# A feed-forward, attention, feed-forward kernel: expert and router products from scaled fp16 parts, norm statistics moved to GpSimd, and every engine's order rewritten

## The reference

```python
x = x + 0.5 * ffn(layernorm(x))        # x: 4 x 1024 x 128, f32
x = x + attn(layernorm(x))
x = x + 0.5 * ffn(layernorm(x))

def ffn(t):                            # 8 experts of 128x128, top 2
    probs = softmax(t @ router_w.T + router_b)
    w = top2(probs) / (sum of the two + 1e-10)
    y_all = einsum('nh,ehd->ned', t, experts)        # every expert
    out = sum over the two chosen of w * y_all / sum(w)
    return out * (1 + sum(w) * 1e-10)

def attn(t):                           # 8 heads of 128, 2 groups of 4 heads, latent keys and values of 32
    q = t @ wq;  k = (t @ wk_down) @ wk_up;  v = (t @ wv_down) @ wv_up
    return softmax(causal(q @ k.T / sqrt(128))) @ v @ wo
```

## Time and profile before

| | |
|---|---|
| median of 3 runs (lowest, highest) | 480.3 us (479.63, 483.49) |
| the profiled execution: its own time, its span | 482.28 us, 480.5 us |
| mean granted PE clock | 0.968 of full speed |
| busy: PE, DVE, ACT, POOL | 439.5, 398.5, 332.2, 300.4 us |

### The profile page before, as it was taken

How to read it: one execution, slowest core, us unless ns; L and a number is a source line. 1 busy time by engine, 2 the same in 40 slices (tenths; PEclk the granted TensorE clock), 3 DMA queues, 4 the chain that set the end, 5 groups by cost and what they waited for, 6 DMA issues and landing times.

```text
span 480.5 us, 10127 instructions
## 1 busy us (share of the span) xinstructions
PE 439.5 (91%) x3294; PEld 241.9 (50%) x3294; DVE 398.5 (83%) x1320; ACT 332.2 (69%) x748; POOL 300.4 (63%) x323
## 2 busy tenths in 40 slices
PE   1796989999899999999999999999899999999962
PEld 0572545444444555645655664655445545543641
DVE  5777799999979889989998988997788898933774
ACT  3356628568588756987986857984895596889433
POOL 3177005249739743697779846597497229999855
PEclk9978889999999999999999999999999999999977
DMA  6100311104001100001120100011011000000001
GB/s 193 35 21 26 83 34 39 34 2 105 2 2 52 35 1 1 2 12 43 33 67 8 34 1 3 29 46 34 13 40 57 1 25 2 1 23 1 24 7 37
DMA packets 21124, 14.52 MB, mean 30 GB/s; under 512 B 2952, under 2 KB 20944, under 8 KB 21072
## 3 DMA queue, kind: packets, MB, share of 16 engines
q1 hardware_dynamic: 21072, 13.88, 10.7%
HBM read 3.78 MB, written 2.10 MB: 12 GB/s over the span
## 4 chain that ended last, share of the span: by engine, by line
PE 69%; DVE 10%; POOL 8%; issue 6%; ACT 4%; DMA 1%; SPq 0%; POOLq 0%; ACTq 0%; DVEq 0%
PE bank L1209 11%; PE bank L1232 11%; PE bank L1254 11%; PE bank L1162 5%; PE bank L1259 5%; PE bank L1163 4%; PE bank L1164 4%; PE bank L1276 3%; PE bank L1180 3%; PE bank L1237 2%; PE bank L1134 2%; POOL sums L620 2%; POOL pair_sum L591 2%; PE bank L1150 2%; PE bank L1173 2%
## 5 line engine op out<-in xcount | busy, mean ns | idle before, releaser
L740 ACT ACTIVATE prob<-bank,exp_scale 128x512 f32<-128x512 f32 x288 | 190.5, 692 | 48.4 <-PE bank L1237 33.4
L620 POOL TENSOR_TENSOR sums<-sums,prob 128x1024 f32<-128x1024 f32 x48 | 112.9, 2372 | 0.7 <-ACT prob L740 0.7
L705 ACT ACTIVATE scaled<-bank,gate 128x128 f32<-128x128 f32 x256 | 80.5, 378 | 42.4 <-PE bank L1164 17.5
L1232 PE MATMUL bank<-q_stack,k_stack 98*128 98x512 f16 (+3 forms) x384 | 103.7, 328 | 3.6 <-DMA q_stack<-mT_lo 1.8
L1209 PE MATMUL bank<-k_stack,q_stack 96*128 96x512 f16 (+3 forms) x384 | 102.2, 329 | 1.7 <-DVE m_fin L956 1.2
L591 POOL TENSOR_TENSOR pair_sum<-dve_sum,scaled 128x256 f32<-128x256 f32 x64 | 46.8, 731 | 74.9 <-DVE dve_sum L943 63.8
L963 DVE TENSOR_REDUCE m_part<-bank 128x1 f32<-128x512 f32 x128 | 83.2, 676 | 5.7 <-PE bank L1209 5.2
L959 DVE CUSTOM_DVE_ANT_0 masked<-bank,mask_qk 128x384 f32<-128x384 f32 (+1 forms) x128 | 76.1, 612 | 5.2 <-PE bank L1209 4.6
L1254 PE MATMUL bank<-prob,v_lat 128*32 128x512 f32 (+3 forms) x768 | 78.4, 492 | 0.1
L1162 PE MATMUL bank<-we_hi,xT_hi 128*128 128x512 f32 x128 | 66.6, 520 | 1.0 <-DVE k_lo L808 0.6
L574 POOL TENSOR_TENSOR rstd<-var_eps,half_power 128x4 f32<-128x4 f32 (+1 forms) x18 | 22.1, 1226 | 64.0 <-DVE neg_mean L857 64.0
(11 more groups left out here) (129 smaller groups left out, 673.3 us busy)
## 6 DMA issues: line engine op xcount, KB each, us to landing
q_stack<-q_hi SPq DMA_DIRECT2D x32, 128.0 KB, 3.0
x<-in_L_attn_x SPq DMA_DIRECT2D x8, 256.0 KB, 3.3
q_stack<-q_lo SPq DMA_DIRECT2D x16, 128.0 KB, 3.2
out_x<-x SPq DMA_DIRECT2D x8, 256.0 KB, 2.3
k_stack<-k_hi SPq DMA_DIRECT2D x16, 64.0 KB, 2.5
we<-in_L_ffn_expert_weights SPq DMA_DIRECT2D x1, 512.0 KB, 4.1
x<-in_L_attn_wq SPq DMA_DIRECT2D x1, 512.0 KB, 6.2
x<-in_L_attn_wo SPq DMA_DIRECT2D x1, 512.0 KB, 7.4
```

The source lines that it names most:

```text
L620: nc.gpsimd.tensor_tensor(into, first if j == 1 else into, new, ALU.add).then_inc(sum_step, 1)
L705: nc.scalar.activation(scaled[:, tile % NTB, i, :], home_of(("y", f, n, 2 * t))[:, i * D:(i + 1) * D], ACT.Copy, scale=gate_of(f, n, t)[:, ...
L740: nc.scalar.activation(prob[:, n % NP, :], bank[ST + n % NST][:], ACT.Exp, scale=exp_scale[:, 0:1]).then_inc(p_ready, 1)
L1232: last = mm(into[:, at:at + CH - off], k_stack[:, b % 2, g, j * P:(j + 1) * P], q_stack[:, c, g * NR + r, off:CH], start=at == 0, stop=not ...
```

## The change

Four things are changed together.

1. The experts' weights and the router's are divided by a unit (their largest absolute value over 16384), the transposed activations (`xn` now holds half the normalised value) are multiplied by 2048, and both are split in two fp16 parts instead of two f32r parts. The triplet stays three products, now fp16; the router becomes three products for each of its four groups in place of two f32 ones. The units are found at the start in 8 new DVE steps (`weight_units`, letter `w`) and 2 new PE steps (`u`), and go back into the result through `y_unit` and `logit_unit`.
2. Of the 7 DVE steps of a norm run 2 stay (the sums); POOL does 7 (`normalisation`) in place of 2.
3. Routing has 23 steps in place of 27, writes its transpose to PSUM, and `merge` is a reduction over one operand. After this no recurring DVE step reads two operands from SBUF, apart from one-column scalars; `low_weights` at the start still does.
4. All five order strings are new. Counts of steps other than the above are the same.

The diff, cut to its core:

```diff
--- before.py
+++ after.py
@@ constants @@
+X_SCALE = 1024.0
+W_SCALE = 16384.0
-STAT_STEPS = 7
-GATE_STEPS = 27
+STAT_STEPS = 2
+NORM_STEPS = 7
+GATE_STEPS = 23
+WEIGHT_STEPS = 8
@@ the five order strings; PE_ORDER ends so @@
-    "1SSVSSz5SSY7SSSVSSY5Sl0SVSSVSV6VVY1Y2Y3Y7J6JJJY5Y0Y1Y2Y3z6l7Y0Y5Y1Y6Y3Y2Y7Y0"
+    "Y5SSVSSVl7SSVSSVSSVSSV1VVY0Y6Y2Y5Y3J1JJJY0Y6Y2Y5Y1Y3Y7Y0z6Y2l1Y5Y6Y3Y7Y0Y2Y1Y5"
@@ buffers @@
-        we_hi = sb("we_hi", [P, NE * D], F32R)
-        we_lo = sb("we_lo", [P, NE * D], F32R)
+        we_hi = sb("we_hi", [P, NE * D], FP16)
+        we_lo = sb("we_lo", [P, NE * D], FP16)
+        rw_hi = sb("rw_hi", [P, DL], FP16)
+        rw_lo = sb("rw_lo", [P, DL], FP16)
-        xT_hi = sb("xT_hi", [P, 4, CH], F32R)
-        xT_lo = sb("xT_lo", [P, 4, CH], F32R)
+        xT_hi = sb("xT_hi", [P, 4, CH], FP16)
+        xT_lo = sb("xT_lo", [P, 4, CH], FP16)
@@ GpSimd: norm_power becomes normalisation @@
-            def norm_power(l, n, chunks, i):
+            def normalisation(l, n, chunks, now):
                 at, run = norm_tiles(l, n, chunks), runs(l, n)
-                if i == 0:
+                g = nc.gpsimd
+
+                def step(i, after, op, *args, **kw):
+                    if i == now:
+                        if after is None:
+                            pool.wait_ge(bn_done[l], (n + chunks) * TC)
+                        else:
+                            pool.wait_ge(norm_step[l], (run - 1) * NORM_STEPS + after + 1)
+                        op(*args, **kw).then_inc(norm_step[l], 1)
+
+                mean_e, mean_o = (stats[:, l, at, k] for k in (1, 4))
+                df, var, r, nm = (a[:, l, at] for a in (diff, variance, half_rstd, neg_mean))
+                minus_half = half_power[:, 0:chunks * TC]
+                step(0, None, g.tensor_tensor, df, mean_e, mean_o, ALU.subtract)
+                step(1, 0, g.tensor_tensor, df, df, df, ALU.mult)
+                if now == 2:
                     pool.wait_ge(stat_step[l], run * STAT_STEPS)
-                    nc.gpsimd.tensor_tensor(rstd[:, l, at], var_eps[:, l, at], half_power[:, 0:chunks * TC], ALU.pow)\
-                        .then_inc(rstd_step[l], 1)
-                else:
-                    pool.wait_ge(rstd_step[l], run * 2 - 1)
-                    nc.gpsimd.tensor_tensor(shift[:, l, at], neg_mean[:, l, at], rstd[:, l, at], ALU.mult)\
-                        .then_inc(rstd_step[l], 1)
+                step(2, 0, g.tensor_scalar, var, var, 4.0 / D, 4.0 * LN_EPS, ALU.mult, ALU.add)
+                step(3, 0, g.tensor_tensor, nm, nm, minus_half, ALU.mult)
+                step(4, 2, g.tensor_tensor, var, var, df, ALU.add)
+                step(5, 4, g.tensor_tensor, r, var, minus_half, ALU.pow)
+                step(6, 5, g.tensor_tensor, shift[:, l, at], nm, r, ALU.mult)
@@ ScalarE @@
-                act.wait_ge(we_loaded, N_DMA)
-                copy(we_hi[:], we[:]).then_inc(we_split, 1)
+                act.wait_ge(weight_step, 6)
+                copy(rw_hi[:], rwT[:], per_w_unit[:, 1:2]).then_inc(we_split, 1)
+                copy(we_hi[:], we[:], per_w_unit[:, 0:1]).then_inc(we_split, 1)
...
-                copy(into, home_of(("xt", l, n))[:]).then_inc(xT_ready[l], 1)
+                copy(into, home_of(("xt", l, n))[:], 2.0 if l == 1 else 2.0 * X_SCALE).then_inc(xT_ready[l], 1)
@@ VectorE: the split and the new weight units @@
-            def low_weights():
-                dve.wait_ge(we_split, 1)
-                V.tensor_tensor(we_lo[:], we[:], we_hi[:].bitcast(F32), ALU.subtract).then_inc(low_split, 1)
-
             def low_transposed(l, n):
                 dve.wait_ge(xT_ready[l], n + 1)
                 home = xt_home(l, n)
-                V.tensor_tensor(xT_lo[:, home, :], home_of(("xt", l, n))[:], xT_hi[:, home, :].bitcast(F32),
-                                ALU.subtract).then_inc(xlo_ready[l], 1)
+                scaled_low(xT_lo[:, home, :], home_of(("xt", l, n))[:], 2.0 * X_SCALE, xT_hi[:, home, :])\
+                    .then_inc(xlo_ready[l], 1)
 
             def scaled_low(dst, src, scale, hi):
                 return V.scalar_tensor_tensor(out=dst, in0=src, scalar=scale, in1=hi, op0=ALU.mult, op1=ALU.subtract)
+
+            def low_weights():
+                dve.wait_ge(we_split, 1)
+                scaled_low(rw_lo[:], rwT[:], per_w_unit[:, 1:2], rw_hi[:]).then_inc(low_split, 1)
+                dve.wait_ge(we_split, 2)
+                scaled_low(we_lo[:], we[:], per_w_unit[:, 0:1], we_hi[:]).then_inc(low_split, 1)
+
+            def weight_units(i):
+
+                seen = bank[OB]
+                if i == 0:
+                    dve.wait_ge(prep_act, 2)
+                    V.tensor_reduce(out=w_peak[:, 1:2], in_=rwT[:, 0:NE], op=ALU.max, axis=AX.X,
+                                    apply_absolute_value=True).then_inc(weight_step, 1)
+                elif i == 1:
+                    dve.wait_ge(we_loaded, N_DMA)
+                    V.tensor_reduce(out=w_peak[:, 0:1], in_=we[:], op=ALU.max, axis=AX.X,
+                                    apply_absolute_value=True).then_inc(weight_step, 1)
...
+                elif i == 4:
+                    dve.wait_ge(weight_pe, 2)
+                    V.tensor_scalar(w_unit[:], seen[:, 0:2], 1.0 / W_SCALE, None, ALU.mult).then_inc(weight_step, 1)
+                elif i == 5:
+                    dve.wait_ge(weight_step, 5)
+                    V.reciprocal(per_w_unit[:], w_unit[:]).then_inc(weight_step, 1)
+                elif i == 6:
+                    V.tensor_scalar(y_unit[:], w_unit[:, 0:1], 0.5 / X_SCALE, None, ALU.mult).then_inc(weight_step, 1)
@@ VectorE: statistics, routing, merge @@
-                def step(i, op, *args, **kw):
-                    if i == now:
-                        if i == 0:
-                            dve.wait_ge(bn_done[l], (n + chunks) * TC)
-                        else:
-                            dve.wait_ge(stat_step[l], (run - 1) * STAT_STEPS + i)
-                        op(*args, **kw).then_inc(stat_step[l], 1)
-
-                mean_e, mean_o = (stats[:, l, at, i] for i in (1, 4))
                 means, squares = (stats[:, l, at, i:i + 4:3] for i in (1, 2))
-                nm, df, ve = neg_mean[:, l, at], diff[:, l, at], var_eps[:, l, at]
-                step(0, V.reduce_sum, nm, means, AX.X)
-                step(1, V.tensor_tensor, df, mean_e, mean_o, ALU.subtract)
-                step(2, V.tensor_tensor, df, df, df, ALU.mult)
-                step(3, V.reduce_sum, ve, squares, AX.X)
-                step(4, V.tensor_scalar, df, df, 0.25, LN_EPS, ALU.mult, ALU.add)
-                step(5, V.scalar_tensor_tensor, out=ve, in0=ve, scalar=1.0 / D, in1=df, op0=ALU.mult, op1=ALU.add)
-                step(6, V.tensor_scalar, nm, nm, -0.5, None, ALU.mult)
+                if now == 0:
+                    dve.wait_ge(bn_done[l], (n + chunks) * TC)
+                    V.reduce_sum(neg_mean[:, l, at], means, AX.X).then_inc(stat_step[l], 1)
+                else:
+                    V.reduce_sum(variance[:, l, at], squares, AX.X).then_inc(stat_step[l], 1)
...
-                step(0, None, V.transpose, g_t[:, 0:nt].rearrange("p t e -> p (t e)"), logits)
-                step(1, 0, V.tensor_tensor, p_l, g_t[:, 0:nt, 0:NE], bias_b, ALU.add)
+                step(0, None, V.transpose, turned, logits)
+                step(1, 0, V.scalar_tensor_tensor, out=p_l, in0=turned.rearrange("p (t e) -> p t e", t=nt)[:, :, 0:NE],
+                     scalar=logit_unit[:], in1=bias_b, op0=ALU.mult, op1=ALU.add)
...
-                step(19, 18, V.reciprocal, r4, r4)
-                step(20, 19, V.tensor_tensor, p_5, p_5, r4, ALU.mult)
-                step(21, 20, V.tensor_scalar, r6, p_5, EPS, 2.0, ALU.max, ALU.mult)
-                step(22, 20, V.tensor_scalar, p_7, p_5, EPS, 1.0, ALU.mult, ALU.add)
-                step(23, 21, V.reciprocal, r6, r6)
-                step(24, 22, V.tensor_tensor, p_7, p_7, r4, ALU.mult)
-                step(25, 24, V.tensor_tensor, p_7, p_7, r6, ALU.mult)
-                if now == 26 and u.index >= 2:
+                step(19, 17, V.reciprocal, p_7, p_5)
+                step(20, 18, V.reciprocal, r4, r4)
+                step(21, 20, V.scalar_tensor_tensor, out=p_7, in0=r4, scalar=EPS, in1=p_7,
+                     op0=ALU.mult, op1=ALU.add)
+                if now == 22 and u.index >= 2:
                     old = (FRONT, BACK)[f][u.index - 2]
                     dve.wait_ge(act_picked, (TILE[f, old.n + old.count - 1, TC - 1] + 1) * HALF)
-                step(26, 25, V.tensor_tensor, gate[:, f, u.index % 2, 0:nt], s_l, per_expert(p_7), ALU.mult)
+                step(22, 21, V.scalar_tensor_tensor, out=gate[:, f, u.index % 2, 0:nt], in0=s_l, scalar=y_unit[:],
+                     in1=per_expert(p_7), op0=ALU.mult, op1=ALU.mult)
...
-                V.tensor_tensor(m_fin[:, Q % 2], m_part[:, Q % 2, 0], m_part[:, Q % 2, 1], ALU.max)\
```

(16 more changed lines are left out.)

128 lines of the change are left out of this document (76 added, 52 removed).

## The result

The changed kernel takes 460.5 us (median of 4 runs, 460.24 to 461.55), beside it the kernel before takes 481.9. The ratio is 0.9575, 95% interval 0.952 to 0.9629: 4.2% faster, where 2.9% was forecast. One of the four executions of the kernel before (487.24 us) was in a slower state of the chip; the ratio is that of the means without it. The profiled execution took 460.24 us with a span of 458.0. The span is 22.5 us shorter, where the sum said 14.0.

A forecast was written before the change was run, and what follows sets the result against it. PE time was taken to bound two thirds of the kernel. Terms 5.5 + 2.5 + 1.4 + 2.0 + 1.0 + 2.5 - 0.9 = 14.0 us came off the 480.3 median: 466.3 us, 2.9% faster, range 460 to 474.

The forecast's parts named there:

- rival (a): Weight loads were exposed after all and waits go with DVE's stalls: 449 us, or likelier halfway, 457; chance 0.13.
- Triplets and router: PE, 60 to 427 us: fp16 saves 0.06 us a triplet (bound 0.155), 5.5 in all; 0.25 a router step, 2.5.
- Triplets elsewhere count at nothing: Triplets outside 60 to 427 us save no time, because chains of single steps hide them.
- Places in the order: Two triplets fewer stand before score step 262, at about 427 us: 1.4 us saved; otherwise no large effect from the order.
- DVE: DVE loses 25 to 30 us of work and stalls; only PE's 5.5 us idle can return: 2.0 us saved.
- POOL: New norm steps of 0.20 us, 18 us in all, hidden if nobody waits; 1.0 us saved in the last quad.
- Start: POOL does chunk 1's norm itself, so its router and the 3.6 us block come earlier: 2.5 us saved, bounds 4 and -2.
- Tail: After the last sum: shorter norm, router and routing against combine steps and a second `yT`: 0.9 us lost.
- (b): POOL takes the gain back: the 12 us of new steps lie on the path, 478 us, within 1%; chance 0.12.
- (c): Slower: the long norm chain on POOL runs late and PE stands still before the transposes, 490 us; chance 0.05.
- (d): Faster products leave PE idle in the middle and its clock falls there, costing 8 us: 474; chance 0.02.
- (e): DVE's stalls stay because another kind of step causes them, costing 2 us: 468; chance 0.68 together with the forecast.

The follow-up runs named there:

- experiment 2: The changed kernel with the five old order strings, edited only where the new arithmetic forces it: 474.7 us, ratio 0.9828 to the kernel before.
- 6: The changed kernel with the merge of the two partial maxima again one step with two SBUF operands: 467.5 us, ratio 0.9682 to the kernel before.
- 7: The kernel before with only the merge of the two partial maxima made a reduction over one operand: 481.5 us, ratio 0.9987 to the kernel before.
- 9: The changed kernel with five more POOL steps, results unused, in each norm run's chain: 480.3 us, ratio 0.9956 to the kernel before.
- 1: The changed kernel with expert products in f32r halves and the router in two fp32 parts again, new orders: 469.6 us, ratio 0.9725 to the kernel before.
- 3: The changed kernel with the old orders and with f32r expert products and fp32 router as before: 483.3 us, ratio 1.0043 to the kernel before.
- 10: The changed kernel with a shorter norm, 6 steps on POOL and 1 on VectorE, orders kept: 460.1 us, ratio 0.9532 to the kernel before.
- 4: The changed kernel with five norm steps of each run back on VectorE in a row, new orders: 472.6 us, ratio 0.9787 to the kernel before.
- 5: The changed kernel with the old orders and five norm steps of each run back on VectorE in a row: 486.8 us, ratio 1.0114 to the kernel before.

## Why the prediction was right, and where it was not

The time lies in the range and on the right side. But it lies at the edge of the forecast's own range (460 to 474), nearer to the 457 of rival (a) than to 466.3, and the total was nearer than its terms. Through one ladder of medians: the kernel before 482.0; with norm, merge, routing and weight unit changed 483.3; with the fp16 parts too 474.7; with the new orders 460.5.

- **Triplets and router**, 5.5 + 2.5 = 8.0: right mechanism, right size. 9.1 measured under the new orders, 8.5 under the old. A router part starts 0.055 us after the one before, as forecast. A triplet gives 0.053 us, near the 0.06 taken, and a router step 0.28, near the 0.25. That the long row of a first f32r product is mostly no PE time was read rightly; the bound of 0.155 was not in play. "Triplets elsewhere count at nothing" holds under the new orders (0.7 of 9.0 us in the start) and not under the old (3.7 of 10.1).
- **Places in the order**, 1.4: here the prediction failed. The step was "I expect no large gain or loss from the order by itself", from nearly equal counts of work before each score. The orders are worth 14.3 us. The traces of the changed kernel and of experiment 2 tell where: the changed kernel is 4.6 us ahead at the first score, 9.3 at exponent 168, 9.4 at exponent 240 (with 80 and 96 triplets done in both) and 14.1 at the end. Runs show 5.7 of the last quad and at most 3 of the start; the 5 us or more between are not split further, and what in the orders wins them stays open. Of the 9.4 us, 6.5 are idle time of PE. I had counted triplets at score 262 (2 fewer), not at the last sum (5 fewer, some 3.5 us); and a count of work says nothing of what each queue waits for.
- **DVE**, 2.0 with a bound of 5.5: PE's idle time in the body fell by 3.2 us, inside the bound, and DVE's 376.5 us busy is near the 372 forecast. The stalls of before are 7.9 us, not "some 9". As a price it was the wrong figure: the merge alone is worth 6 to 7 us under the new orders and none under the old ones (6, 7).
- **POOL**, "18 us hidden", and 1.0 saved in the last quad: the steps' 0.20 us is right. Under the new orders the first dose did stay hidden (2.0 us of PE idle in the body), and a second one does not (9). That this owes to orders laid with the first dose in mind is argued, not shown. In the last quad the new orders save 5.7 us, not 1.0; the timelines point to the order of POOL's steps, of which I had counted the number.
- **Start**, 2.5: 4.6 came, past the bound of 4, with 1.3 us between executions of the same start (6). `w_unit` at 12.64 is as forecast (12.5), `xn` at 15.81 is 0.8 later (15) and the first triplet at 16.20 is 1.2 later (15). The upT products at 20.92 take 1.97 us and not 3.6: PE's granted clock between 20 and 30 us is 1.00, where it was 0.66. And the old orders with the same steps show no gain at the first score, so it was laid out, not won by the move of the norm.
- **Tail**, 0.9 lost: 0.7 saved, with five more triplets in it.
- **Rivals.** (a) named nearly the right size (457) by the wrong mechanism: the weight loads were not exposed (1), and DVE's relief with its stalls gave nothing under the old orders (3, 7). (b) and (c) name a true danger, for a second dose costs 19.8 us, though in the body PE then waits at the scores and not before the transposes; the first dose did not show. (d) PE's clock in the body stayed 1.00. (e) no: the stalls are gone, and they do come from steps with two SBUF operands, and from `tensor_scalar`.

So the time fell within the range in part by luck, because two errors of opposite sign met: norm, stalls, routing and start gave nothing under the old orders where I had 4.6, and the orders gave 14.3 where I had 1.4. Right by its mechanism was only the term of the products. Under the new orders each removal has its own price (9.1, 14.3, 12.1, 7.1 and 5.6 us); they add up to 48 and not to the 21 of the whole, so none of them is a share of the gain.

## What to carry to other kernels

When every engine follows a written order, work that is added can cost its whole length even on an engine that is not full. Work taken away was given back here only on PE, the engine that is full; a DVE stall and single steps on DVE and POOL gave nothing (7, 10). Lay the orders again, then measure. Price an edit under both orders, the old and the new, before it is called the cause. Small VectorE steps with two SBUF operands, and `tensor_scalar` ones, don't belong beside long GpSimd steps; a reduction over one operand does the same merge without the wait, though in the kernel before that alone gained nothing.

## What the runs showed of the hardware beyond what was expected

A DVE step of 4 elements with one SBUF operand and a constant stalled as long (2.31 us) as one with two operands (2.27 us). In the kernel before and in experiments 4 to 7 each stalled step ended 0.02 to 0.09 us after a POOL step did, short POOL steps of 0.46 us included, and POOL's sums kept their length (2.33 to 2.39 us). The same merge as a reduction, beside the same sums, never took over 0.19 us.
